# All row statistics ahead of the key projection, and the softmax of the next block ahead of new scores, in a pre-norm attention and expert layer

## The reference, cut to what matters

```python
x = L0_attn_x                                   # (8, 2048, 1024) f32
# layernorm(x) = (x - mean) / sqrt(var + 1e-5), over the last axis
h = _layernorm(x)
q, k, v = h @ Wq, h @ Wk, h @ Wv                # 1024 x 1024 each
s = where(causal, q @ k.T, -inf) / sqrt(1024)
x = x + softmax(s) @ v
h = _layernorm(x)
w = top-2 of 8 sigmoid router scores, scaled to sum 1, 0 elsewhere
x = x + shared(h) + sum_e w[:, e] * expert_e(h)
# shared and each expert: (silu(h @ gate) * (h @ up)) @ down, inner width 2048
```

## Time and profile before

| What | Value |
|---|---|
| timed runs | 3568.31 and 4247.85 us, median 3908.08 |
| profiled execution | 3572.03 us |
| its span, slowest core | 3570.5 us (cores: 3556.6 to 3570.5) |
| mean granted TensorE clock of the cores | 0.979 to 0.981 |
| TensorE busy | 3335.1 us, 93% |
| ScalarE busy | 562.1 us, 16% |
| VectorE busy | 751.5 us, 21% |

### The profile page before, as it was taken

How to read it: one execution, slowest core, us unless ns; L and a number is a source line. 1 busy time by engine, 2 the same in 40 slices (tenths; PEclk the granted TensorE clock), 3 DMA queues, 4 the chain that set the end, 5 groups by cost and what they waited for, 6 DMA issues and landing times.

```text
span 3570.5 us, 40624 instructions; the slowest of 8 cores (3556.6 to 3570.5 us)
## 1 busy us (share of the span) xinstructions
PE 3335.1 (93%) x15655; PEld 1549.4 (43%) x15960; DVE 751.5 (21%) x1195; ACT 562.1 (16%) x1068; POOL 285.6 (8%) x336
## 2 busy tenths in 40 slices
PE   2597768999999999999999999999999999999999
PEld 1255333444444444444444444444444444444444
DVE  1202432221221222222212222122222122222222
ACT  2434441010101010101111010101010101111010
POOL 0000001000101010101001000101010101001000
PEclk9699988999999999999999999999999999999999
DMA  6012006442825292537246442816282536246442
GB/s 142 1 24 25 1 1 88 55 58 37 112 31 72 31 123 30 77 48 94 36 59 87 55 60 36 116 26 76 31 118 34 72 51 92 37 59 92 86 71 60
DMA packets 327625, 214.54 MB, mean 60 GB/s; under 512 B 6928, under 2 KB 301840, under 8 KB 327440
## 3 DMA queue, kind: packets, MB, share of 16 engines
q0 software_dynamic: 323024, 195.14, 41.4%
q1 hardware_dynamic: 4416, 16.78, 1.4%
HBM read 398.63 MB, written 8.39 MB: 114 GB/s over the span
## 4 chain that ended last, share of the span: by engine, by line
PE 91%; DVE 3%; issue 3%; DMA 2%; ACT 2%; DVEq 0%; POOL 0%; ACTq 0%; POOLq 0%
PE psE L694 14%; PE psC L651 14%; PE psD L651 14%; PE psF L694 14%; PE psB L641 14%; PE psA L641 14%; DMA WBUF<-wk 1%; PE psC L479 1%; PE psD L479 1%; DVE KBUF L673 1%; DVE R L495 1%; ACT XQ L250 1%; PE psA L281 1%; DVE lst L197 1%; PE psA L383 0%
## 5 line engine op out<-in xcount | busy, mean ns | idle before, releaser
L641 PE MATMUL psA<-XQ,WBUF 128*128 128x512 bf16 x2256 | 543.0, 381 | 11.7 <-DVE KBUF L673 6.1
L651 PE MATMUL psC<-XQ,WBUF 128*128 128x512 bf16 x2256 | 542.3, 380 | 2.5
L641 PE MATMUL psB<-XQ,WBUF 128*128 128x512 bf16 x2259 | 540.4, 379 | 2.4
L651 PE MATMUL psD<-XQ,WBUF 128*128 128x512 bf16 x2261 | 540.2, 379 | 2.3
L694 PE MATMUL psE<-VBUF,KBUF 128*128 128x512 bf16 x2261 | 518.1, 379 | 22.7 <-DVE KBUF L673 20.5
L694 PE MATMUL psF<-VBUF,KBUF 128*128 128x512 bf16 x2254 | 516.8, 379 | 2.6
L664 ACT ACTIVATE gscr<-psA 128x512 bf16<-128x512 f32 x288 | 171.9, 597 | 1792.4 <-PE psA L641 1553.8
L673 DVE TENSOR_TENSOR KBUF<-gscr,psC 128x512 bf16<-128x512 bf16 x288 | 198.0, 688 | 804.0 <-PE psC L651 739.4
L673 DVE TENSOR_TENSOR KBUF<-gscr,psD 128x512 bf16<-128x512 bf16 x288 | 198.0, 688 | 792.6 <-PE psD L651 773.9
L694 PEld LDWEIGHTS psE<-VBUF,KBUF 128*128 128x128 bf16 x2304 | 224.1, 98 | 296.3 <-issue 28.6
L641 PEld LDWEIGHTS psA<-XQ,WBUF 128*128 128x128 bf16 x2304 | 225.8, 98 | 283.5 <-issue 14.2
(11 more groups left out here) (134 smaller groups left out, 1069.5 us busy)
## 6 DMA issues: line engine op xcount, KB each, us to landing
WBUF<-gw POOLq DMA_DIRECT2D x128, 512.0 KB, 6.0
WBUF<-uw POOLq DMA_DIRECT2D x128, 512.0 KB, 7.9
VBUF<-dw POOLq DMA_DIRECT2D x32, 1024.0 KB, 14.8
R<-x SPq DMA_DIRECT2D x4, 2048.0 KB, 24.6
WBUF<-sgwT POOLq DMA_DIRECT2D x16, 512.0 KB, 6.1
WBUF<-suwT POOLq DMA_DIRECT2D x16, 512.0 KB, 8.2
out<-R SPq DMA_DIRECT2D x16, 512.0 KB, 2.6
VBUF<-sdwT POOLq DMA_DIRECT2D x4, 1024.0 KB, 18.8
```

The source lines that it names most:

```text
L641: ts=ts, gb=gb, tbase=tbase: e.matmul(gb[:, :], wgrp[:, pp, 0, hc, ic * 128:(ic + 1) * 128], XQ[:, hc, tbase + ts * 512: tbase + (ts + 1) ...
L651: ts=ts, ub=ub, tbase=tbase: e.matmul(ub[:, :], wgrp[:, pp, 1, hc, ic * 128:(ic + 1) * 128], XQ[:, hc, tbase + ts * 512: tbase + (ts + 1) ...
```

## The change

Two loops are written in another order. No instruction is added, removed or altered in size.

```diff
+    for tt in range(NTT):
+        ln_stats(tt, v_pre=0, v_dx=t_xc[tt // 4])
     qkv_banks = (psA, psB, psC, psD)
     bi = 0
     wait("tensor", dWw, t_wk)
     xq_ready_s = 0
     for ts in range(4):
         for tt4 in range(4):
             tt = 4 * ts + tt4
-            ln_stats(tt, v_pre=0, v_dx=t_xc[tt // 4])
-        for tt4 in range(4):
-            tt = 4 * ts + tt4
             ln_fin_a(tt)
@@
     for qi in range(NTT):
+        if qi + 1 < NTT:
+            emit_softmax(qi + 1)
         if qi + 2 < NTT:
             emit_scores(qi + 2)
         tok_pv = emit_ptpv(qi)
-        if qi + 1 < NTT:
-            emit_softmax(qi + 1)
         pv = emit_epilogue(qi, tok_pv)
```

## The result

The changed kernel is 0.66% slower than the kernel before: the ratio of their times is 1.0066, with a 95% interval of 1.0039 to 1.0092 (20 timed runs of one, 19 of the other). The medians over all of these runs are 3607.35 and 3587.05 us. Many runs of either kernel are lengthened by a lower clock on the cores of a die and are left out of the ratio, which is also why the median of two runs given at the top, 3908.08, says nothing about the change. 0.66% of 3570 us are 24 us. The forecast of 3591 against 3572 was 19 us, a ratio of 1.0053: the right sign, and inside the interval. The change is clear of noise, since the interval leaves out 1, but far under two per cent.

The account below looks back on a forecast made before the run. TensorE is busy 93% of the span, but in the two changed stages the ScalarE and VectorE chain sets the time. -13.4 + 25.7 + 7 = +19 us on 3572.03 gave 3591 us, range 3575 to 3612.

Parts of the forecast that it names:

- start of TensorE: Before the first transposition: 12 more tiles' statistics need the last quarter of x, so TensorE starts 2.0 us later.
- three seams: Between key projection groups: Ln no longer stands behind four squares, 5.15 us less at each seam, 15.45 us in all.
- waiting behind the exponential: Attention: score and probability copies wait for the exponential (17.7 us) and its VectorE hand-over (7.4 and 0.6), 25.7 us.
- clock: Attention: longer waits make TensorE's clock fall more, 3.4 plus 4.3 us, taken as 7, bounds 0 and 25.
- its own sign: The prediction called itself wrong if the attention stage does not get longer by 25 to 35 us.
- Part one: Layer norm 1 and key projection: row statistics of all 16 tiles come first, -15.45 + 2.0 = -13.4 us.
- Part two: Attention loop: the exponential of row block qi+1 moves to the front of iteration qi, costing 25.7 us before clock.
- if a quarter of the ten other long iterations does this: Attention clock: a quarter of ten iterations get a half-clock stretch twice as long, 2.5 x 1.7 = 4.3 us.
- Rival 2: Attention: the clock falls for two stretches in every iteration, 25 us instead of 7, so 3609 us; chance 12%.
- that rule alone: Attention clock by the skill's rule: every burst after a wait starts low, two more bursts, 3.4 us instead of 7.
- Rival 1: Attention: the moved exponential is absorbed, leaving only the gain of 13.4 us, so 3559 us; chance 8%.
- Rival 3: Start and key projection: moving the statistics ahead brings nothing, so 3605 us; chance 7%.

Follow-up runs that it names:

- e1: Kernel before with only the statistics of all 16 tiles moved first, softmax in its old place; ratio 0.9963 (0.9933 to 0.9994).
- e7: Changed kernel with 18 useless matmuls before the first score-bank wait, iterations 6 to 13; attention stage 250.8 to 251.7 us on four cores, 267.9 to 268.4 on others.
- e8: Kernel before with 9 useless matmuls before the wait for the first score bank; attention stage 222.9 to 225.3 us on all cores.
- e4: Changed kernel with each exponential run twice in its new place; attention stage 289.6 us, against 268.0 in the changed kernel.
- e2: Kernel before with only the softmax of block qi+1 moved ahead of the scores of qi+2; ratio 1.0083 (1.0048 to 1.0119).
- e3: Kernel before with each exponential run twice in its old place; attention stage 231.2 us, against 232.2 before.
- e9: Kernel before with the next group's statistics put between a group's normalization and its key matmuls, softmax in its old place; ratio 0.9946 (0.9904 to 0.9988).
- e5: Changed kernel with VectorE's maximum and scaling directly behind their block's score operations, only the exponential at the front; attention stage 257.5 us, against 268.0.
- e11: Changed kernel with the layer norm of a finished block written one iteration later, as in e10; attention stage 204.9 us.
- e10: Kernel before with a finished block's layer norm written one iteration later, in front of the epilogue; attention stage 185.4 us, ratio 0.9882 (0.9742 to 1.0021).
- e12: Kernel before with the diffs of e9 and e10 together, softmax in its old place; ratio 0.9799 (0.9744 to 0.9853).

## What the prediction had right, and the step that failed

| Term | forecast, us | measured, us | from |
|---|---|---|---|
| start of TensorE | +2.0 | +1.9 (e1: +2.0) | table of stages |
| three seams | -15.45 | -16.9 (e1: -17.3) | table of stages |
| waiting behind the exponential | +25.7 | +22.9 | waits before and after |
| clock | +7 | +13 | TensorE's busy time before and after; 9 of it by e7 and e8 |
| last epilogue to first expert matmul | none | +0.5 | stretch and table of stages |
| sum | +19 | +21.4 as a mean of the cores, +24 by the ratio | |

The mechanism was right in both parts. The step that failed is the size of the clock term: 7 us were forecast, 13 measured. By its own sign the prediction is wrong by a little, since the attention stage was to get longer by 25 to 35 us and got longer by 36.4. That the sum is only 2 us off is partly luck: the clock was 6 us too low, the waiting 2.8 too high, and the seams brought 1.5 more than said.

**Part one** came as worked out: 5.13 us of wait gone in the seam (5.15 said), TensorE's start at 52.40 (52.8 said). That the mean start is later by 1.9 us where 2.0 were said is closer than the measurement allows: with the old order the mean start is 48.6 to 49.8 us in five runs, with all statistics first 50.0 to 51.5 in seven. In the seams the waits account for the forecast alone: on core 0 TensorE's 15 waits for the normalization fall from 53.1 to 37.8 us, 15.3 less. The 1.5 us more are for the most part in the work: on the six cores of which all records are there, TensorE's busy time in the key stage is 193.3 us before and 192.0 after, and 63 to 67 us of that stage were at half clock before, 43 to 50 after. The prediction had no clock term for this stage.

**Part two, the waiting.** The step from the row of the exponential to the delay of the score copy was right: 2.30 us measured in iteration 12 of the timeline for a forecast of 0.57 + 1.79 = 2.36, and e4 gives the slope of one. Of the two terms, the wait for VectorE's scaling was sized at 0.57 us and is 0.38 in most iterations and 1.39 in iteration 2, 5.8 us in all for 7.4 forecast. The sum was 2.8 us too high. In the eight iterations with a score bank it is nearly right (38.1 - 22.3 = 15.8 us for a forecast of 16.8). In the others the waits grew by 7.1 for a forecast of 8.9. A possible reason, not shown, is that TensorE, at low clock, was still working there for a part of the time that ScalarE came later, so that the delay shows as longer work.

**The clock** is the term that was mis-sized: 13 us instead of 7. The step that failed is "if a quarter of the ten other long iterations does this". Two iterations that had a full clock before lost it, as said, but each got two stretches at half clock and not one. And of the six that had one stretch before, five got a second. The iteration from the epilogue of block 12 to that of block 13, in the kernel after:

```profile
487.60:509.60 22.00, 16.48 (x86) 7.49 (x83) 7.29 (x14) 8.65 (x20) 0.00 (x0) 0.84 0.00 0
```

A clock of 0.84 over 22.0 us are 7.0 us at half clock, where the iteration of the earlier trace rows, one block earlier, with 0.91 had 3.3. Of the eight iterations with a wait for a score bank seven have 6.8 to 7.1 us and one has 3.4: nearly all, not a quarter, got a second stretch. Together they have 51.5 us at half clock instead of 20.5, and the seven others 37 instead of 24. The attention had some (1 - 0.88) x 2 x 209.6 = 50 us at half clock before and (1 - 0.81) x 2 x 245.5 = 93 us after. 43 us more at half clock would cost 21 if TensorE worked all through them; it lost 13, the rest lies in its waits. Rival 2 had what happened nearly right: from iteration 5 on, ten of eleven have two stretches. But its price, 25 us, was farther off than the forecast, because it counted no waiting. Of the Trainium skill's rule in "TensorE: Matmul & The Clock Gate", section on HAM oscillation, that every burst behind such a wait starts at the low clock, the changed kernel's waits agree better than the kernel before's: no iteration has a clock above 0.89, where two had 1.00. But the sum by that rule alone, 3.4 us, was farther off than mine.

**The rivals.** Rival 1 (absorbed) is out by e2 and e4. It is right in one respect, which the forecast shared: ScalarE has time enough, and e3 shows that even twice the exponentials fit, in the old place. Rival 3 (the hoist brings nothing) is out by e1.

**What remains open:** how many of the 2 us at the start e9 wins back, what is left of the cost of the front place when VectorE's two operations come early and the layer norm late, why a longer wait is followed by two stretches at half clock and a shorter one by one or none, and the third clock level.

## What to carry to other kernels

- A busy share says nothing of a place in an in-order queue. The same exponentials cost nothing in one place when doubled (e3), and one for one in another (e4). Before an instruction is moved up, look at what stands directly behind the new place and who waits for that.
- A small operation that an instruction depends on has to move with it, and not behind a third one: 10.5 of 36 us came from VectorE's two operations of 0.15 us standing behind the normalization (e5), and behind the epilogue they cost again (e11).
- When TensorE waits for a chain, look for the member of the chain that nobody needs soon. Here it was the layer norm of a finished block: written one iteration later, it took the waits for a score bank and most of the low clock out of the attention (e10, e12), for more than 40 us.

## What was not expected of the hardware

Some cores of some runs have a clock of about 0.81, neither of the two levels that the other rows show, over a long dense stretch of 100 to 160 us. In e7 cores 2 to 5 had it through most of the attention. In e1 core 3 had it at the beginning of the experts, and core 0 of the same execution did not. The view by windows of e1, columns as in the earlier trace rows, first of core 3:

```profile
560.00:590.00 30.00, 30.00 (x116) 12.41 (x115) 4.81 (x7) 4.19 (x7) 5.05 (x6) 0.81 0.97 124
```

and of core 0:

```profile
560.00:590.00 30.00, 29.27 (x135) 13.19 (x136) 6.19 (x9) 4.78 (x8) 5.04 (x6) 1.00 1.13 155
```

It cost core 3 some 20 us (2975.8 us of experts against 2955 to 2958 on the cores without it), as much as the whole change; in e10, where it lasted 160 us, it cost 30. It came in pairs of cores, in e1 (2 and 3), e8 (2 and 3), e9 (6 and 7), e10 (4 and 5) and e11 (0 and 1), and in none of the profiled executions of the kernel before, the changed one and e12. A time of the slowest core that is 20 us high can be this, and is then no property of the kernel; the stages of an undisturbed core are.
